# Two-head value-output products, longer row runs, singly placed early work and a written-out VectorE loop in a fused decoder layer

## The reference

```
x = x + selfattn(LN(x))        # 16 heads of 16, scores[0,-1] and scores[-1,0] masked, softmax, Wo
x = x + tanh(gate) * (xattn(LN_g(x), ctx) @ w_out + b_out)     # 16 heads of 64, 64 context rows
t = LN(x)
a  = entmax15(LN(t @ proj))                        # 16 experts
h  = gelu(((t,1) @ Win1 * (a @ C1)) @ Wout1.T)     # rank 128, 1024 wide
x  = x + ((h,1) @ Win2 * (a @ C2)) @ Wout2.T
```

## Time and profile before

| | |
|---|---|
| three runs | 1076.5, 1081.06, 1083.22 us, median 1081.06 |
| the profiled execution | 1082.92 us, span 1081.11 us, granted clock 0.973 |
| TensorE busy | 1007.7 us, 93% of the span |
| VectorE busy | 769.6 us, 71% |
| ACT busy | 622.3 us, 58% |
| POOL busy | 148.4 us, 14% |
| first exp of batches 0 to 7 | 79.0, 194.5, 291.5, 411.0, 529.1, 646.2, 765.4, 883.1 us |
| last exp | 983.1 us |

### The profile page before, as it was taken

How to read it: one execution, slowest core, us unless ns; L and a number is a source line. 1 busy time by engine, 2 the same in 40 slices (tenths; PEclk the granted TensorE clock), 3 DMA queues, 4 the chain that set the end, 5 groups by cost and what they waited for, 6 DMA issues and landing times.

```text
span 1081.1 us, 16488 instructions
## 1 busy us (share of the span) xinstructions
PE 1007.7 (93%) x5354; PEld 582.1 (54%) x5354; DVE 769.6 (71%) x1608; ACT 622.3 (58%) x860; POOL 148.4 (14%) x175
## 2 busy tenths in 40 slices
PE   5899998999989999899999999999999998999897
PEld 4444433546544745465555645564556654566676
DVE  3557564788788768966798668976797678636774
ACT  2346665654646666565657664676557665754533
POOL 2000000012011300121002200120012101211320
PEclk9899998999989999999999998999999999899999
DMA  6588676643230142111421051113311140021001
GB/s 160 135 232 257 195 214 179 176 147 108 53 115 7 25 142 75 50 31 30 167 69 29 10 179 37 40 30 94 122 49 29 30 167 21 1 79 65 14 1 40
DMA packets 91306, 97.41 MB, mean 90 GB/s; under 512 B 10564, under 2 KB 76807, under 8 KB 89191
## 3 DMA queue, kind: packets, MB, share of 16 engines
q1 hardware_dynamic: 91238, 96.63, 30.3%
HBM read 41.34 MB, written 29.36 MB: 65 GB/s over the span
## 4 chain that ended last, share of the span: by engine, by line
PE 68%; DVE 19%; issue 5%; SPq 3%; ACT 2%; DMA 2%; POOL 1%; DVEq 0%; ACTq 0%; POOLq 0%
PE y_ps L949 22%; PE x_ps L949 16%; PE pv_ps L949 8%; PE sm_ps L949 7%; PE st_ps L949 7%; DVE mx L1573 6%; PE y_ps L1109 3%; PE y_ps L1076 2%; SPq L806 2%; DVE stat L1593 1%; DMA pt<-in_L_xattn_w_out 1%; PE x_ps L1038 1%; DVE res L1645 1%; DVE xt_lo L1563 1%; DVE xn L1613 1%
## 5 line engine op out<-in xcount | busy, mean ns | idle before, releaser
L1573 DVE TENSOR_REDUCE mx<-sm_ps 128x2 f32<-128x1024 f32 x256 | 312.7, 1222 | 120.3 <-PE sm_ps L949 114.8
L1377 ACT ACTIVATE probs<-st_ps 128x1024 f32<-128x1024 f32 x256 | 261.7, 1022 | 164.8 <-PE st_ps L949 150.0
L949 PE MATMUL pv_ps<-probs,v_all 128*32 128x512 f32 x1024 | 138.2, 619 | 0.2 <-ACT o_t L1377 0.2
L949 PE MATMUL sm_ps<-k_st,q_st 50*128 50x512 f32 x512 | 122.7, 474 | 12.8 <-DVE mx L1573 5.0
L949 PE MATMUL st_ps<-q_st,k_st 52*128 52x512 f32 x512 | 122.0, 472 | 5.8 <-ACT probs L1377 5.5
L949 PE MATMUL x_ps<-b_cat,pt 128*128 128x256 f32 x448 | 114.0, 388 | 0.1
L949 PEld LDWEIGHTS sm_ps<-k_st,q_st 50*128 50x128 f32 x512 | 49.2, 188 | 108.7 <-DVE mx L1573 46.6
L949 PEld LDWEIGHTS st_ps<-q_st,k_st 52*128 52x128 f32 x512 | 48.9, 187 | 87.7 <-issue 42.9
L949 PEld LDWEIGHTS x_ps<-b_cat,pt 128*128 128x128 f32 x448 | 80.2, 189 | 22.5 <-issue 8.7
L949 PE MATMUL y_ps<-a_cat,xt_hi 128*128 128x512 f32 x244 | 84.3, 427 | 4.5 <-DVE xt_lo L1563 4.1
L685 POOL TENSOR_TENSOR px<-px,cst 128x512 f32<-128x512 f32 x56 | 58.0, 1043 | 200.9 <-DVE cst L1668 200.9
(11 more groups left out here) (308 smaller groups left out, 1722.9 us busy)
## 6 DMA issues: line engine op xcount, KB each, us to landing
a_scr<-a_cat SPq DMA_DIRECT2D x32, 512.0 KB, 5.0
a_cat<-a_scr SPq DMA_DIRECT2D x8, 2048.0 KB, 7.8
q_st<-qk_hi SPq DMA_DIRECT2D x128, 64.0 KB, 2.3
k_st<-qk_hi SPq DMA_DIRECT2D x128, 64.0 KB, 2.3
b_scr<-b_cat SPq DMA_DIRECT2D x8, 1024.0 KB, 5.9
b_cat<-b_scr SPq DMA_DIRECT2D x8, 1024.0 KB, 9.7
xa<-in_x SPq DMA_DIRECT2D x9, 512.0 KB, 3.8
q_st<-qk_lo SPq DMA_DIRECT2D x64, 64.0 KB, 2.3
```

Of the source, the lines that this page charges most:

```text
L949: return nc.tensor.matmul(dst, lhs, rhs, start=start, stop=stop, **kw)
L1377: return nc.scalar.activation(dst, src, f, **kw)
L1573: nc.vector.tensor_reduce(mx[:, c % 2, :].rearrange("p (m x) -> p m x", m=2)[:, :, col], sm_ps[:], axis=AX, op=ALU.max).then_inc(sm_taken, 1)
```

## The change

1. Value-output products: the units are taken by two, (7, 8) and (9, 10). The second one issues four matmuls with a contraction over 64 rows and 128 output rows (two batches at once); head 0 goes to the first bank of y_ps, head 1 to the second. Eight matmuls of two units become four. The first unit of the two issues nothing, so both banks are held until the second.
2. The layouts of a_cat and of its scratch put the high and low parts of a head pair side by side: store_a becomes 16 transfers with row runs of 1 KB instead of 32 of 512 B, the scores read a_cat in four blocks of 128 columns. The scratch of b_cat is laid out by context row; load_b becomes two transfers.
3. The hand-written work of the start becomes units of its own (b = -2) in the EARLY tables, V tiles among them; the casts of the small weights are one unit for VectorE, placed in batch 1, and their loads move from the start's load list into EARLY_SP, as do the mask rows. The V tiles wait for w_v alone. The EARLY_* tables, PE_TASKS, ACT_TASKS, DVE_TASKS, LAST_* and TAIL_* have new orders.
4. VectorE's loop over batches 3 to 6 is written out; the other engines keep theirs.
5. The closing half of the feed forward part of the last batch uses a bank of sm_ps, and the table loads of the last batches have outputs of their own.

```diff
-    (0, "PV", 15, 0), (0, "M", 0, 0), (0, "V", 0, 0), (0, "V", 0, 1), (0, "V", 1, 0), (0, "V", 1, 1), (0, "X1", 0, 0),
+    (0, "M", 0, 0), (0, "V", 0, 0), (0, "V", 0, 1), (0, "V", 1, 0), (0, "V", 1, 1), (0, "X1", 0, 0), (0, "TN", 0, 0),
+    (0, "PV", 15, 0), (2, "M", 1, 0), (2, "X1", 1, 0), (2, "OT", 0, 0), (4, "M", 2, 0), (4, "QK", 0, 0),
...
 EARLY_PE = (
-    (-1, "M", 16, 0), (-1, "SW", 0, 0), (-1, "SW", 1, 0), (0, "SW", 0, 0), (-1, "M", 17, 0), (0, "SW", 1, 0),
+    (0, "SW", 0, 0), (-2, "SW", 0, 0), (-2, "SW", 1, 0), (-2, "SW", 2, 0), (-2, "SW", 3, 0), (-2, "SW", 4, 0),
...
 EARLY_SP = (
-    ("XA", 1, 0), ("FS", 0, 0), ("LD", 0, 0), ("LD", 1, 0), ("FS", 0, 1), ("SA", 0, 0), ("SA", 0, 1), ("FS", 0, 2),
+    ("SM", 0, 0), ("LD", 0, 0), ("RW", 0, 0), ("RW", 1, 0), ("XA", 1, 0), ("FS", 0, 0), ("FS", 0, 1), ("LD", 1, 0),
+    ("SA", 0, 0), ("FS", 0, 2), ("SA", 0, 1), ("LD", 2, 0), ("SB", 0, 0), ("MR", 0, 0), ("SA", 1, 0), ("SA", 1, 1),
...
-        a_cat = sb("a_cat", [P, 2, KT, INNER], F32R)
+        a_cat = sb("a_cat", [P, PAIRS, KT, 2, P], F32R)
...
+                for j in range(2):
+                    sp.dma_start(b_cat[XD * j:XD * j + XD], b_scr[g.row()].rearrange("a s h f -> (a s) h f")
+                                 [:, :, D * j:D * j + D]).then_inc(b_in, 16)
...
             def store_a(p, m):
                 s_taken(sp, setup_no(p, 3 + 2 * m))
                 s_taken(sp, setup_no(p, 4 + 2 * m))
-                for part in range(2):
-                    sp.dma_start(a_scr[:, :, part, m, P * p:P * p + P].rearrange("b p c -> p b c"),
-                                 a_cat[:, part, m, :].bitcast(F32).rearrange("p (b c) -> p b c", b=B)
-                                 ).then_inc(as_out, 16)
+                sp.dma_start(a_scr[:, :, p, m].rearrange("b p e c -> p b e c"), a_cat[:, :, m].bitcast(F32)).then_inc(as_out, 16)
...
+            def setup_in(n):
+
+                if n < IN_O1:
+                    pe.wait_ge(wvo_in, 16 * 2)
+                    setup_w(4 + n - IN_W)
+                elif n < IN_V:
+                    pe.wait_ge(wout_in, 16 * 2)
...
+                else:
+                    if n == IN_V:
+                        s_taken(pe, w_unit(4))
+                        s_taken(pe, w_unit(5))
+                    y = s_fill(pe, setup_no(-2, n))
+                    v_tile(y, n - IN_V, 0)
+                    v_tile(y, n - IN_V, 1)
...
-                if n >= 7:
-                    for b2 in range(2):
-                        bb = 2 * (n - 7) + b2
+                if n >= 7 and (n - 7) % 2 == 1:
+                    banks = (y_ps[:, setup_no(p, n - 1) % 2], y)
+                    for i in range(2):
+                        bb = n - 8 + i
                         for j in range(2):
                             hd = slice(XD * j, XD * j + XD)
-                            last = mm(y[hd, D * b2:D * b2 + D], kv_t[hd, p % 2, 1, SK * bb:SK * bb + SK], t[hd, 3, :],
-                                      True, True, tile_position=(XD * j, XD * j))
-                    last.then_inc(y_full, 1)
+                            last = mm(banks[j][:, D * i:D * i + D], kv_t[hd, p % 2, 1, P * bb:P * bb + P], t[hd, 3, :],
+                                      True, True)
+                            if i == 1:
+                                last.then_inc(y_full, 1)
...
-            pe.wait_ge(w_in, 16 * 18)
-            for n in range(4, 8):
-                setup_w(n)
-            setup_wout()
-            pe.wait_ge(small, 8)
...
-            pe.wait_ge(rows_in, 16 * 12)
...
             iteration(At(None, 2))
-            with dve.Fori(3, B - 1) as it:
-                iteration(At(it, 0))
+            for n in range(3, B - 1):
+                iteration(At(None, n))
```

More of the change, by code:

```diff
@@ L1137, in router @@
                 if t == 0 or t == 2 and is_last(g):
+                    if g.reg is None and g.off == 0:
+                        pe.wait_ge(small, 8)
                     fill(pe, g, "PJ", pj, after=[("X3", t + k) for k in range(KT)])
@@ L1148, in z1 @@
             def z1(g, n):
+                if g.reg is None and g.off == 0 and n == 0:
+                    pe.wait_ge(small, 8)
                 y = fill(pe, g, "Z1", n, after=[("X3", j + (KT * n if is_last(g) else 0)) for j in range(KT)])
```

224 lines of the change are left out of this document (123 added, 101 removed), and 507 rows, old and new, of tables (ACT_TASKS, DVE_TASKS, EARLY_ACT, EARLY_DVE).

## The result

The changed kernel takes 1041.3 us (median of 4 runs, 1038.27 to 1045.59) against 1078.95 (4 runs, 1076.5 to 1083.22): ratio 0.965, 95% interval 0.961 to 0.969. The profiled executions are 1041.88 and 1082.92 us, 41.0 apart. The forecast was 1056 with 1038 to 1076 as its range; the time lies in the range, but outside the forecast's own 1046 to 1066, at the 1042 of rival R1.

A forecast was written before the change was run, and what follows sets the result against it. TensorE was taken to set the time nearly everywhere. Gains of 7.5 + 12.5 + 1 + 3 + 1 = 25 us took the profiled 1082.9 to 1057.9, 1056.0 against the median; range 1038 to 1076.

The forecast's parts named there:

- R1: Steady iterations: first part shortens by all that leaves VectorE, switches cost nothing; 2 to 4 us each, 1042 us; chance 0.13.
- A, the start: Start to first exp: shorter waits for V tiles and pair 2's weights, shorter value-output units; 7.5 us gain, 3 to 10.
- B, batch 0: Batch 0's stretch: value-output couples 9.0 us, fewer switches 2.5, transfers 1; 12.5 us gain, 4 to 17.
- R2: Setup: both banks end together, next y product waits for ACT's copies; 14 us gain, 1067 us; chance 0.15 with R5.
- R5: Value-output products: the doubled contraction runs its halves one after the other; B is 4, sum 1064 us; chance 0.15 with R2.
- C, batch 1: Batch 1: same number of matmuls on TensorE; 1 us gain for the order, 0 to 3.
- D, the steady iterations: Batches 2 to 6: written-out loop and new orders; 3 us gain for the five, ends -9 and +6.
- The back edge at 0.6: VectorE's loop, batches 3 to 6: of 1.43 us idle an edge, 0.6 counts and the rest is caught up.
- The orders at +1.2 for the second part and -0.8 for the first: Steady iteration: from S 0 on 1.2 us longer by moved matmuls and three switches; before S 0 0.8 shorter on VectorE.
- E: Last batch and tail: own bank for the closing products and a new order; 1 us gain, 4 either way.
- R3: Steady iterations: three more switches, first part no shorter; +2.5 us each over five, 1072 to 1077 us; chance 0.11.
- R4: Steady iterations: EN 0 behind M 31 and PJ 3 delays AT and H; 39 us over five, 1100 us; chance 0.06.

The follow-up runs named there:

- experiment 5: Changed kernel with the old value-output products and b_cat's former layout, stores and loads: 1051.1 us, ratio 0.972 to the kernel before.
- experiment 10: Changed kernel, loop written out, with EN 0 and PJ 3 ahead of M 31 again: 1041.9 us, ratio 0.962 to the kernel before.
- experiment 8: Changed kernel with H 2 of batches 2 to 6 behind S 2 again (behind EX 2 on ACT): 1067.2 us, ratio 0.987 to the kernel before.
- experiment 9: Changed kernel with VectorE's loop kept and LN1A 2 and 3 moved behind EN 0: 1054.0 us, ratio 0.975 to the kernel before.
- experiment 2: Kernel before with only VectorE's loop written out: 1073.9 us, ratio 0.994 to the kernel before.
- experiment 4: Kernel before, loop kept, with only the new PE_TASKS, ACT_TASKS and DVE_TASKS: 1073.6 us, ratio 0.994 to the kernel before.
- experiment 7: Changed kernel with the second store of head pair 0 ahead of the third stack fill: 1038.0 us, ratio 0.960 to the kernel before.
- experiment 12: Changed kernel with pair 0's second store ahead of the third stack fill, measured beside the unmodified changed kernel: 1039.0 us, ratio 0.959 to the kernel before.
- experiment 6: Changed kernel with the former layout of a_cat and its scratch (32 transfers of 512 KB): 1047.5 us, ratio 0.969 to the kernel before.
- experiment 1: Changed kernel with VectorE's hardware loop over batches 3 to 6 put back: 1053.5 us, ratio 0.974 to the kernel before.
- experiment 11: The changed kernel itself, unmodified, measured once more: 1042.9 us, ratio 0.964 to the kernel before.
- experiment 3: Changed kernel with the old PE_TASKS, ACT_TASKS and DVE_TASKS (batches 2 to 6): 1057.5 us, ratio 0.978 to the kernel before.

## Why the prediction came out as it did

**The whole.** The direction and the range held, the mechanism only in part, and that the time lies in the range owes something to luck. What was forecast for the value products came (7.5 and 1.0 us in experiment 5). What decided the size were two things that the sum did not have: the interplay of the order and the written-out loop (15.0 us over five iterations, forecast 3), and the clock (up to 15.7). By its own signs the forecast was wrong: it named iterations over 2 us off today's, and they are 3.0 shorter; it had 116 to 118 us without clock loss, and they take 114.1. R1, with 0.13, has the time and the size an iteration (2 to 4 us), and it was right that the edge is paid in full; the rest of its mechanism, that everything that leaves VectorE's first part counts, fails for M 31 (experiment 10).

**A, the start: wrong.** 7.5 us forecast, none came. The wait for the pair's weights did leave the chain, as the term said. The V tiles shrank from 5.49 to 4.91, though between 36 and 40 us the clock is 0.56 before and 0.76 after, so that may be the clock's. TensorE's idle time between 28 us and the first exp, of which the term wanted to take 2.7, rose instead, from 5.5 to 8.8: its busy time fell from 45.5 to 42.4, and the saving went into new waits. I asked only what SP issues ahead of the load and not what else it issues late: the store of pair 0 behind twelve stack issues. And the clock is lower there (0.83 against 0.87), which the sum left out. At like clocks (0.86 and 0.87) the first exp is at 76.5 to 78.4 in experiments 8 to 10 and at 77.9 to 79.1 in the three profiles with the old start (the kernel before, experiments 2 and 4), so the start gained about 1 us. Experiments 7 and 12 give 3.9 back by moving one entry, most of it with the clock.

**B, batch 0: right in sum, 14.3 against 12.5, and partly by luck.** The value products measured 7.5 where the term had 9.0 (experiment 5). The layout measured 4.6 where it had 1 for the transfers (experiment 6); 3.4 of that is idle time of TensorE, the rest goes with a clock of 0.98. The clock was not in the sum: the stretch had 0.97 before and 1.00 after, by these shares up to 3.5 us of 115.5 (an estimate). 7.5, 3.4 and 3.5 make 14.4 already, so nothing is left that would show the 2.5 for the switches; no run tested them by themselves. R2 and R5 fell: the couple takes 0.8 to 1.1 us. The Trainium skill's remark on tiling and the reading of banks ("TensorEngine Tiling (Array Packing)", PSUM Bottleneck) is borne out in small, 2.7 us of TensorE's idle time against 10.2 of work saved, and not as the bound. The Trainium skill's 512 B for the full rate ("DMA: Bandwidth & Descriptors", Specifications) is not borne out for this pattern: 512 KB with runs of 512 B land in 5.0 us, 1024 KB with runs of 1 KB in 5.6.

**C, batch 1: wrong by 4.** The larger part is the clock: in experiment 9, with the same early orders and the same 545 records on TensorE, batch 1 takes 97.2 us at a clock of 1.00; here it takes 100.0 at 0.97. But 97.2 at 1.00 is no gain over the 97.0 that the kernel before needed at 0.98; with one fall worth 0.8 to 1.5 in that, the new early part costs batch 1 some 1.0 to 1.7 us, an estimate. What in it does is open.

**D, the steady iterations: the step that failed.** Two sizes were wrong.

The back edge at 0.6. I read it off batch 3, the only iteration before that follows a written-out one, as 48.4 against 49.0. That control was not clean. From the first exp to S 0 batch 3 had 48.1 us before and batch 4 had 48.7; in experiment 2, behind the very same batch 2, batch 3 has 47.2, and batches 4 to 6 have 46.8 to 47.3. VectorE's timelines of batch 3 agree within 0.05 us up to one instruction, which took 2.28 us before and 0.68 in experiment 2; from the next M on, all is 0.9 late. In the kernel before POOL was at work on a long instruction for most of that time:

```profile
448.53 1.89 POOL L1999 TENSOR_TENSOR xo<-res,table_pad 128x1024 f32<-128x1024 f32 x1 [18.29 <-DMA out_x<-xo]
448.68 2.28 DVE L1563 TENSOR_TENSOR z_lo<-zbuf,z_hi 128x512 fp32r<-128x512 f32 x1
```

```profile
447.50 0.68 DVE L1563 TENSOR_TENSOR z_lo<-zbuf,z_hi 128x512 fp32r<-128x512 f32 x1
```

In experiment 2 POOL's instruction starts at 447.99, behind the start of z_lo. That POOL holds VectorE up is argued from these times, not tested. So the one iteration without an edge was long for another reason, and the comparison hid most of the edge's price. The edge is worth 1.5 (experiment 2), not 0.6. I had the row with 1.43 and let one iteration talk me out of it.

The orders at +1.2 for the second part and -0.8 for the first. Measured without edges they are -0.2 (68.4 to 68.2) and -1.3 (47.2 to 45.9). The count of matmuls and switches was no measure of the second part. M 31's exchange with EN 0, which carried most of my term for the first part, is worth nothing (experiment 10). By the list of TensorE's waits, those before S 0 (0.84), before M's (0.26 and 0.34) and before score products (0.46 and 0.30) of experiment 2's kernel are gone, 2.2 together, and one of 0.87 for z_lo is new. Which entry of the tables removed each was tried for H 2 only: without it the 0.84 is back (experiment 8). In the old order z_lo also takes 1.56 us in batch 4, beside POOL again, and 0.69 in the new one, where behind S 0 another short instruction takes 0.81 in place of 0.17 (L1654, at 581.28) beside another one of POOL; what that is worth no run shows.

What I did not see at all is that the two parts depend on each other. I priced the edge in the old order and added the orders' gain. The edge is some 3.3 to 3.6 us from the start of M 31 in the old order (645.88 to 649.18 in the earlier trace rows) and of EN 0's last part in the new one (507.95 to 511.52 in experiment 1, 622.70 to 626.23 in experiment 9). That both are the moment from which the branch counts is read from the equal lengths; the profile shows a wait at M 31 only. In the old order M 31 and two LN1A ran in that time and hid 1.9 of it; the new order moved both elsewhere, and with the loop it gains nothing (117.4 against 117.1). Written out, that price is gone altogether.

Of the 21.6 us, 3.0 an iteration are 15.0. The rest goes with the clock: batches 2, 3, 5 and 6 before were 2.4, 1.0, 2.1 and 0.6 over batch 4, at clocks of 0.96 to 0.99, together 6.1. After the change they run at 1.00. What TensorE did before a fall is in part in the profiles: its idle time between the first exp and S 0 was 5.1 to 6.3 us an iteration before and is 2.8 to 4.1 now. Of the twelve iterations behind an edge (the kernel before, experiments 1, 4 and 9) eight have a clock under 1.00; of batches 4 to 6 in the changed kernel and experiments 2, 5 to 7 and 10 to 12, all without a loop, none has (experiment 3 has one, experiment 8 with its table loads three). So the falls come with the longer waits, but not by their length alone: batch 4 before has 6.1 us of them at a clock of 1.00. Whether fewer waits keep the clock up is not shown.

**E: wrong by 7.** Batch 7 went from 100.0 us at a clock of 0.97 to 95.1 at 1.00; by these shares up to 3.0 of the 4.9 are the clock's. With the steady orders alone it is 95.8, also at 1.00 (experiment 4), and with its own new orders behind the old steady ones 101.1 at 0.93 (experiment 3), so what the orders themselves gave can't be told from these. The tail is 98.0 before, 97.3 with the old orders in experiment 4, 95.6 with the new ones in experiment 3 and 94.6 here: most of the 3.4 is its own orders and its new bank, which no run separates.

R3 and R4 fell: no iteration grew, and EN 0 behind M 31 delays nothing.

## What to carry to other kernels

A loop's edge has no fixed price: here it is 3.3 to 3.6 us from a point shortly before the branch, and what is queued behind that point hides a part; so a new order and a written-out loop are priced together, or one of them looks worthless. A control taken from one iteration of the same trace needs a second one: compare the two instruction by instruction, since one stretched instruction can hide the whole effect. Compare only stretches of the same granted clock; here the clock was up to 15.7 of the 41.0 us, and it moved the start, batches 0 and 1 and the last one by as much as the terms under test. And when a queue's order changes, follow each store and load through it, not only the one that was late before.
